# Biases of the attention's q, k and v taken off TensorE, in a three-layer decoder block on one core

## The reference

```
def _L0_attn_ref(x, Wq, bq, Wk, bk, Wv, bv, Wo, bo):
    q = (x @ Wq.T + bq).reshape(B, S, H, D)
    k = (x @ Wk.T + bk).reshape(B, S, H, D)
    v = (x @ Wv.T + bv).reshape(B, S, H, D)
    ...            # rotary turn of q and k by position
    qk = jnp.einsum('bshd,bstd->bsht', q, k) / jnp.sqrt(jnp.float32(D))   # heads against heads, per token
    att = jax.nn.softmax(qk, axis=-1)
    out = jnp.einsum('bsht,bstd->bshd', att, v)
    ...
    return out @ Wo.T + bo

x = _layernorm(x + _L0_attn_ref(x, ...))                  # attention
x = _layernorm(x + _L0_xattn_ref(x, ctx, ctx, ...))       # mLSTM over ctx: gates, decay matrix D, q-k product, norm
x = _layernorm(x + _L0_ffn_ref(x, ...))                   # 8 experts, one chosen per token, low rank
```

## Time and profile before

| | us |
|---|---|
| median of three runs | 1596.8 (1593.08 to 1603.48) |
| the profiled execution: its own time | 1598.22 |
| its span | 1596.5 |
| PE busy | 1506.4 (94%) |
| DVE busy | 1278.2 (80%) |
| ACT busy | 947.1 (59%) |
| POOL busy | 629.7 (39%) |
| mean granted TensorE clock | 0.973 of full |

### The profile page before, as it was taken

The page is one execution under the profiler, slowest core; times in us unless marked ns, Lnnn a source line. Parts: engine busy times, 40 slices in busy tenths (PEclk is TensorE's granted clock), DMA queues, the critical chain, the costliest instruction groups (busy, mean ns, idle before and its releaser), DMA issues.

```text
span 1596.5 us, 67819 instructions
## 1 busy us (share of the span) xinstructions
PE 1506.4 (94%) x27277; PEld 1194.9 (75%) x27404; DVE 1278.2 (80%) x3337; ACT 947.1 (59%) x2897; POOL 629.7 (39%) x975
## 2 busy tenths in 40 slices
PE   6889999999999999999999999999999999999964
PEld 5677777777777877777787777777777777777742
DVE  6567787788888888888888888888888888888764
ACT  3354656656665665666566566656656665665652
POOL 2233434434434443443444344344444434434431
PEclk8999999999999999999999999999999999999965
DMA  6232433333434333343333334333333433433310
GB/s 206 81 101 84 132 105 101 120 111 100 132 103 118 109 116 109 104 132 103 113 113 113 111 105 132 102 114 113 112 112 105 131 102 106 122 112 112 86 68 27
DMA packets 195143, 174.71 MB, mean 109 GB/s; under 512 B 141887, under 2 KB 143551, under 8 KB 186890
## 3 DMA queue, kind: packets, MB, share of 16 engines
q1 hardware_dynamic: 195082, 173.87, 36.3%
HBM read 139.76 MB, written 34.08 MB: 109 GB/s over the span
## 4 chain that ended last, share of the span: by engine, by line
PE 73%; DVE 18%; issue 5%; ACT 4%; DVEq 0%; POOL 0%; POOLq 0%
PE bank L386 13%; PE bank L387 12%; PE bank L389 12%; PE bank L378 6%; PE quad L440 5%; PE quad L453 5%; PE bank L548 5%; PE quad L500 4%; PE bank L482 4%; PE bank L535 4%; DVE w_sum L950 2%; DVE neg_max L941 2%; DVE ex L946 2%; DVE st L971 2%; ACT Hs L686 2%
## 5 line engine op out<-in xcount | busy, mean ns | idle before, releaser
L679 ACT ACTIVATE Dx<-Mb,a_col 128x128 f32<-128x128 f32 x1024 | 317.7, 388 | 4.1 <-DMA Mb<-m_rows 4.1
L820 POOL TENSOR_TENSOR ex<-ex,w_rec 128x512 f32<-128x512 f32 x64 | 67.1, 1048 | 510.7 <-DVE w_rec L955 510.7
L825 POOL TENSOR_SCALAR_AFFINE_SELECT Dx<-Dx 128x512 f32<-128x512 f32 x256 | 167.5, 679 | 88.4 <-ACT Dx L679 88.4
L1015 DVE SCALAR_TENSOR_TENSOR Dx<-quad,Dx 128x512 f32<-128x512 f32 x256 | 158.7, 681 | 4.4 <-POOL Dx L825 4.1
L721 ACT ACTIVATE ln<-ve 128x1 f32<-128x1 f32 x192 | 38.1, 199 | 197.0 <-DVE ve L976 197.0
L839 POOL TENSOR_TENSOR r<-r,lns_sb 128x512 f32<-128x512 f32 x64 | 82.6, 1290 | 173.2 <-DVE r L1038 106.2
L649 ACT ACTIVATE x1T<-bank 128x512 f32<-128x512 f32 x64 | 38.3, 599 | 149.0 <-PE bank L378 149.0
L386 PE MATMUL bank<-wq_high,x_high 128*128 128x512 f32 x256 | 115.1, 450 | 10.5 <-DVE wq_low L1161 8.5
L386 PE MATMUL bank<-wv_high,x_high 128*128 128x512 f32 x256 | 114.0, 445 | 1.5 <-issue 1.3
L386 PE MATMUL bank<-wk_high,x_high 128*128 128x512 f32 x256 | 114.0, 445 | 0.0
L453 PEld LDWEIGHTS quad<-PT,VG 32*32 32x32 f32 x8192 | 74.9, 103 | 51.9 <-issue 51.2
(11 more groups left out here) (164 smaller groups left out, 4168.5 us busy)
## 6 DMA issues: line engine op xcount, KB each, us to landing
Mb<-m_rows SPq DMA_DIRECT2D x64, 1024.0 KB, 4.7
xb<-in_x SPq DMA_DIRECT2D x256, 64.0 KB
cb<-in_ctx SPq DMA_DIRECT2D x64, 256.0 KB, 2.7
xr<-in_x SPq DMA_DIRECT2D x64, 256.0 KB, 2.7
v_rows<-v_sb SPq DMA_DIRECT2D x64, 256.0 KB, 2.4
VG<-v_rows SPq DMA_DIRECT2D x64, 256.0 KB, 3.9
out_dram<-yo SPq DMA_DIRECT2D x64, 256.0 KB, 2.8
Dx<-in_wq SPq DMA_DIRECT2D x4, 256.0 KB, 3.7
```

What stands on the lines that cost most here:

```text
L679: last = go(Dx[t.parity()][:, j, n, :], Mb[t.parity()][:, h, :], ACT.Exp, bias=a_col[t.parity()][:, h:h + 1], scale=-1.0)
L825: nc.gpsimd.affine_select(Dx[t.parity()][:, j], Dx[t.parity()][:, j], compare_op=ALU.is_ge, fill=0.0, base=0, pattern=[[0, CH], [1, P]], c ...
L1015: stt(out=Dx[t.parity()][:, j], in0=quad[:, j, :].rearrange("p (c n) -> p c n", n=P), scalar=float(D) ** -0.5, in1=Dx[t.parity()][:, j], o ...
```

## The change

- The bias matmuls are gone. For q and k, ACT writes the bias (spread over the 128 partitions in new tables `bias_bc`) into bank 4 ahead of the product (`p_seed_q`, `p_seed_k`), and the product's first matmul adds to what stands there (`first` is False). For v, the product starts its own accumulation, and POOL adds the bias to v_sb in place (`p_vb`); `store_v` waits for that.
- k moves from bank 6 to bank 4, so q and k of a tile use bank 4 in turn: seed of k waits for `QT_sb`, seed of the next q for `KT_sb`.
- F moves from bank 4 to bank 7 and in PE's order from after x1T to before QK; QK stands ahead of k.
- The wait for Hs moves from Y to O.
- `r_y` moves from DVE to POOL; POOL's r_r2 goes from the start of the next step to behind r_y2. On DVE the step ends with C x4 and then KT, and x_shift goes before a_x1.
- In the prologue: no splitting of the biases on DVE, three broadcast loads of 256 KB instead of three of 2 KB, 105 warm-up matmuls (into bank 4) instead of 68.

```diff
-WARM = 68
+WARM = 105
...
             def store_v(t):
-                sp.wait_ge(s.v_sb, upto(t))
+                sp.wait_ge(s.vb_sb, upto(t))
...
-            def bias(b, n):
-                mm(bank[b][:], ones_bf[:], bias3[:, n * E:(n + 1) * E], start=True, stop=False)
...
             def p_q(t):
...
                 pe.wait_ge(s.xlow_sb, upto(t))
-                edge(pe, t, (s.xhigh_sb, 0), (s.QT_sb, 1), (s.fn1_sb, 5))
-                bias(4, 0)
+                pe.wait_ge(s.seedq_sb, upto(t))
+                edge(pe, t, (s.xhigh_sb, 0))
                 product(4, x_high, x_low, 0, False).then_inc(s.q_ps, 1)
 
             def p_k(t):
...
-                pe.wait_ge(s.x2T_sb, upto(t, 4))
-                edge(pe, t, (s.xhigh_sb, 0), (s.xlow_sb, 0), (s.Hs_sb, 3), (s.y3_sb, 6), (s.LT_sb, 6))
-                bias(6, 1)
-                product(6, x_high, x_low, 1, False).then_inc(s.k_ps, 1)
+                pe.wait_ge(s.seedk_sb, upto(t))
+                edge(pe, t, (s.xhigh_sb, 0), (s.xlow_sb, 0))
+                product(4, x_high, x_low, 1, False).then_inc(s.k_ps, 1)
 
             def p_v(t):
...
-                bias(7, 2)
-                product(7, x_high, x_low, 2, False).then_inc(s.v_ps, 1)
+                product(7, x_high, x_low, 2, True).then_inc(s.v_ps, 1)
 
             def a_S(t):
-                for j in range(4):
-                    pe.wait_ge(s.C_sb[j], upto(t, 2))
+                pe.wait_ge(s.KT_sb, upto(t))
...
             def a_O(t):
                 pe.wait_ge(s.pads_set, PADS)
+                pe.wait_ge(s.Hs_sb, upto(t, 2))
...
             def m_gate(t):
-                pe.wait_ge(s.v_sb, upto(t, -1))
+                pe.wait_ge(s.fn1_sb, upto(t, 3))
...
             def x_F(t):
+                pe.wait_ge(s.v_sb, upto(t, -4))
                 pe.wait_ge(s.x2T_sb, upto(t))
-                pe.wait_ge(s.QT_sb, upto(t, -4))
...
-                    last = mm(bank[4][:, 0:NW], x2T[:, c, :], wx_sb[:, c, :], start=(c == 0), stop=(c == CH - 1))
+                    last = mm(bank[7][:, 0:NW], x2T[:, c, :], wx_sb[:, c, :], start=(c == 0), stop=(c == CH - 1))
...
             def x_Y(t):
                 pe.wait_ge(s.LT_sb, upto(t))
-                pe.wait_ge(s.Hs_sb, upto(t, -3))
...
             # PE step
                 if b.real():
                     a_proj(b)
+                if e.real():
+                    x_F(e)
+                if c.real():
+                    m_QK(c)
                 if a.real():
                     p_k(a)
-                if c.real():
-                    m_QK(c)
                 if b.real():
                     m_x1T(b)
-                if e.real():
-                    x_F(e)
                 if f.real():
                     x_LT(f)
...
             # ACT: p_seed_q first in the step, p_seed_k behind r_sq
+            def p_seed_q(t):
...
+                act.wait_ge(s.KT_sb, upto(t, 1))
+                go(bank[4][:], bias_bc[0][:], ACT.Copy, scale=float(D) ** -0.5).then_inc(s.seedq_sb, 1)
+
+            def p_seed_k(t):
...
+                act.wait_ge(s.QT_sb, upto(t))
+                go(bank[4][:], bias_bc[1][:], ACT.Copy).then_inc(s.seedk_sb, 1)
...
             # POOL: p_vb first in the step; r_y, r_y2, r_r2 before x_nm
+            def p_vb(t):
...
+                pool.wait_ge(s.v_sb, upto(t))
+                pool.wait_ge(s.acol_sb, upto(t, 2))
+                tt(v_sb[:], v_sb[:], bias_bc[2][:], ALU.add).then_inc(s.vb_sb, 1)
+
+            def r_y(t):
+                pool.wait_ge(s.hrs_sb, upto(t))
+                pool.wait_ge(s.x2_sb, upto(t, 1))
+                tt(r2[:].rearrange("p (c j d) -> p c j d", j=4, d=D),
+                   Hs[:, :, 0:P].rearrange("p c (j d) -> p c j d", d=D),
+                   h_rs[:].rearrange("p (c j) -> p c j", j=4).unsqueeze(3).broadcast_to([P, CH, 4, D]),
+                   ALU.mult).then_inc(s.y1_sb, 1)
...
             # DVE step
-                if d.real():
-                    r_y(d)
                 if b.real():
                     a_r1(b)
                     a_stats(b)
+                if e.real():
+                    x_shift(e)
+                if b.real():
                     a_x1(b)
+                if c.real():
+                    for j in (1, 3, 0, 2):
+                        m_C(c, j)
                 if a.real():
                     p_KT(a)
-                if c.real():
-                    for j in (1, 3, 0, 2):
-                        m_C(c, j)
-                if e.real():
-                    x_shift(e)
```

More of the change, by code:

```diff
@@ L240, in bass_decoder @@
             ve3_sb ln3_sb rs3_sb nm3_sb yo_sb""".split()
-        four = "Dx_sb Dm_sb C_sb w_in".split()
+        four = "Dx_sb Dm_sb C_sb w_in b_in".split()
         two = "x_in c_in r_in mb_in v_in".split()
@@ L251, in bass_decoder @@
                 [Mb[1][:, 4 * c:4 * c + 4, :].rearrange("p g n -> p (g n)") for c in range(CH)]]
-        bias_in = [t[0:1, :] for t in (y3[0], y3[1], yo)]
-        bias_rest = [t[0:1, :] for t in (x1[0], x1[1], x2[0])]
-        firsts = [(id_sb[:], ident), *[(bias_in[n], bqkv[:, n * E:(n + 1) * E]) for n in range(3)]]
         consts = [
@@ L379, in transposes @@
                 return last
-            def bias(b, n):
-                mm(bank[b][:], ones_bf[:], bias3[:, n * E:(n + 1) * E], start=True, stop=False)
             def product(b, high, low, n, first):
                 for c in range(CH):
-                    mm(bank[b][:], high[:, c, :], w_high[n][:, c, :], start=first and c == 0, stop=False)
-                    mm(bank[b][:], high[:, c, :], w_low[n][:, c, :], start=False, stop=False)
+                    mm(bank[b][:], high[:, c, :], w_high[n][:, c, :], start=first and c == 0, stop=False, skip_group_check=True)
+                    mm(bank[b][:], high[:, c, :], w_low[n][:, c, :], start=False, stop=False, skip_group_check=True)
                 for c in range(CH):
-                    last = mm(bank[b][:], low[:, c, :], w_high[n][:, c, :], start=False, stop=c == CH - 1)
+                    last = mm(bank[b][:], low[:, c, :], w_high[n][:, c, :], start=False, stop=c == CH - 1,
+                              skip_group_check=True)
                 return last
@@ L421, in p_v @@
                     pe.wait_ge(s.low_set, 2)
-                    pe.wait_ge(s.bias_step, 10)
                 pe.wait_ge(s.acol_sb, upto(t, 2))
                 edge(pe, t, (s.xhigh_sb, 0), (s.xlow_sb, 0))
-                bias(7, 2)
-                product(7, x_high, x_low, 2, False).then_inc(s.v_ps, 1)
+                product(7, x_high, x_low, 2, True).then_inc(s.v_ps, 1)
             def a_S(t):
-                for j in range(4):
-                    pe.wait_ge(s.C_sb[j], upto(t, 2))
-                edge(pe, t, (s.QT_sb, 0), (s.KT_sb, 0), (s.Ohigh_sb, 1), (s.Olow_sb, 1))
+                pe.wait_ge(s.KT_sb, upto(t))
+                edge(pe, t, (s.QT_sb, 0), *[(s.C_sb[j], 2) for j in range(4)], (s.Ohigh_sb, 1), (s.Olow_sb, 1))
                 for w in range(4):
@@ L477, in m_gate @@
             def m_gate(t):
-                pe.wait_ge(s.v_sb, upto(t, -1))
+                pe.wait_ge(s.fn1_sb, upto(t, 3))
                 pe.wait_ge(s.x1T_sb, upto(t))
+                edge(pe, t, (s.v_sb, -1))
                 edge(pe, t, (s.cT_sb, 0), (s.acol_sb, 1), (s.Hs_sb, 2))
@@ L557, in _ @@
             pe.wait_ge(s.center_set, 2)
-            for _ in range(WARM):
-                mm(bank[5][:, 0:P], ones_bf[:], ones_bf[:], start=True, stop=True)
+            for n in range(WARM):
+                last = mm(bank[4][:, n % 4 * P:(n % 4 + 1) * P], ones_bf[:], ones_bf[:], start=(n == 0), stop=True,
+                          skip_group_check=True)
+            last.then_inc(s.warm_ps, 1)
             pe.wait_ge(s.center_set, 12)
-            pe.wait_ge(s.first_in, FIRST_IN)
+            pe.wait_ge(s.first_in, 16)
             def step(a):
@@ L842, in r_r2 @@
                 pool.wait_ge(s.y2_sb, upto(t))
-                pool.wait_ge(s.x1_sb, upto(t, -1))
+                edge(pool, t, (s.x1_sb, 0))
                 tt(r2[:], r2[:], x1[t.parity()][:], ALU.add).then_inc(s.r2_sb, 1)
@@ L905, in step @@
                 if c.real():
+                    r_y(c)
                     r_y2(c)
+                    r_r2(c)
                 if f.real():
@@ L1060, in x_shift @@
                 edge(dve, t, (s.L_sb, 1), (s.fn2_sb, 1))
-                tt(fz[:], bank[4][:, 0:2 * nw], wx_shift[:, 0:2 * nw], ALU.subtract).then_inc(s.fz_sb, 1)
-                stt(out=f_n1[:], in0=bank[4][:, 2 * nw:NW], scalar=-2.0, in1=wx_shift[:, 2 * nw:NW],
+                tt(fz[:], bank[7][:, 0:2 * nw], wx_shift[:, 0:2 * nw], ALU.subtract).then_inc(s.fz_sb, 1)
+                stt(out=f_n1[:], in0=bank[7][:, 2 * nw:NW], scalar=-2.0, in1=wx_shift[:, 2 * nw:NW],
                     op0=ALU.mult, op1=ALU.add).then_inc(s.fn1_sb, 1)
```

65 lines of the change are left out of this document (26 added, 39 removed).

## The result

The changed kernel takes 1625.2 us (median, 1624.9 to 1625.8), beside 1597.1 for the kernel before: a ratio of 1.0171, 95% interval 1.0149 to 1.0193. The forecast was 1600, its range ended at 1620. It is slower, by more than the 1% that was set as the bound. Of the rivals C came near in time (1623), but not by what happened.

A forecast was written before the change was run, and what follows sets the result against it. PE, busy 94%, was taken to bound the kernel. From 1598.2, +6 for steps, +1.5 start and -3 tail gave 1602.7, 1601 as median, stated as 1600; the forecast's own range was 1584 to 1614, the overall range 1578 to 1620.

The forecast's parts named there:

- Rival C: POOL's longer queue ahead of the masks delays m_C and KT by 0.4 a step: 1623 us, chance 0.05.
- The three parts of a step: PE's step cut at S, v's first matmul and the projection's end: 9.50, 6.05 and 7.88 us.
- The bare price of bank 5: Between the transpositions of x1 and the next x, without F as cover: a new PE wait of 0.79 a step.
- The Hs wait: PE's wait before Y on ACT's Hs goes and doesn't come back at O: 0.28 a step.
- the seed of k fits: ACT's write between sq and f_e, in a gap of 0.50, sticks out by 0 to 0.1 us.
- v's bias on POOL costs nothing: A 1.29 us operation on POOL; v is read back only for O, so PE shows no delay.
- The start: 37 more warm-up matmuls against no bias splitting on DVE: +1.5 us, bounds 0 and +3.7.
- The tail: The last tile's r_y starts earlier on POOL than on DVE: -3 us, bounds -5 and 0.
- the large terms (0.51 and 0.28 against 0.79 and 0.10): Per PE step: bias matmuls save 0.51, Hs wait 0.28; bank 5 costs 0.79, and the step grows 0.10.
- rival B: Mb's load lands late, delaying Dx, v_sb and F: 0.27 more a step at a 5.1 landing, 1616 us, chance 0.14.
- "58 steps: +6": Filled part, about 130 to 1490 us: 58 steps of 23.43 instead of 23.33, +6 us, between -8 and +12.
- the order "KT, seed of q, x_high": The seed of q delays ACT's copy of x by about 0.4, covered as q comes 2.6 after S: no cost.

The follow-up runs named there:

- e2: The kernel before with F moved ahead of k in PE's queue, nothing else; 1640.6 us, one run.
- e11: The kernel before with only the Hs wait moved from Y to the O product of the next step; 1579.0 us, ratio 0.9881.
- e5: The changed kernel with v's bias on POOL behind the three masks and r_r2 at the head of the next step; 1630.8 us, ratio 1.0210.
- e18: e11 with 8 steps written out in place of 10; 1582.4 us, ratio 0.9905.
- e13: The kernel before with the biases of q, k and v left out and 98 warm-up matmuls in place of 68; 1585.5 us, ratio 0.9902.
- e8: The kernel before with 105 warm-up matmuls in place of 68, nothing else; 1895.2 us, one run.
- e10: The changed kernel with x1's transposition inside k, v's bias behind POOL's masks and x_high ahead of the seed of q; 1582.3 us, ratio 0.9904.
- e3: The changed kernel with 68 warm-up matmuls in place of 105; 1847.7 us, ratio 1.1572.
- e12: The changed kernel with 113 warm-up matmuls in place of 105; 1631.2 us, one run.
- e6: The changed kernel with r_y back on DVE, ahead of r1; 1732.5 us, ratio 1.0814.
- e16: e10 with 121 warm-up matmuls in place of 105; 1652.9 us, one run.
- e1: The changed kernel with x1's transposition between k's eighth and ninth matmul; 1629.5 us, ratio 1.0208.

## Why the prediction was wrong

**Right.** The three parts of a step within 0.04 each. The bare price of bank 5 (e2: 0.81, forecast 0.79). The Hs wait (e11: 0.30, forecast 0.28). That the seed of k fits and that v's bias on POOL costs nothing in the step as long as bank 5 sets it (e5).

**Right in number, not shown or by luck.** The start (+1.0, forecast +1.5): e2, e11 and e18 start as the kernel before does and reach tile 3 at 102.8, 105.8 and 104.1 where it takes 106.2, so +1.0 is within the scatter. The tail (-2.4, forecast -3): the last tile's r_y does start 2.4 earlier behind h_rs and r2 is 2.1 earlier, but from h_rs to the end it is 28.3 instead of 29.0 (29.0 also in e2, e11 and e18, all with r_y on DVE). So the move is worth 0.7; the other 1.7 lie ahead of h_rs, where e11 has 4.2 less than before.

**Mis-sized: the step.** The forecast had 23.43, with 0.10 over before and +6 for 58 steps. The shortest steps are 23.50 to 23.52. Three rests of 0.02, 0.04 and 0.03 add to 0.09, as much as the whole forecast difference: the sum of the large terms (0.51 and 0.28 against 0.79 and 0.10) nearly cancels, so its error rules. One of those terms is sized by e13: the bias matmuls are worth 0.45 a step, not 0.51. Over the loop's 50 steps the shortest step gives +10 where 5 was said. On top come 4 us by which the mean exceeds it, 3 of them in the steps in which F waits for v_sb. That is rival B, priced at 16 more for a landing of 5.1 in every step and given 0.14. B's limit of 4.83 was taken at F's first matmul; the weight load ahead of it already waits from about 4.6, below the median of 4.7. And a spread around the limit strikes every second step; it isn't all or nothing.

**Failed: "58 steps: +6".** This step took the steady step for all tiles from about 130 us on. Tiles 3 to 12 took 14.0 more, about 13 of it unforecast. The trace of before already had it: these nine steps take 8.7 more than nine of 23.32, with 9.8 us of "issue" stops, and I read no row of that stretch. (The 0.73 on "issue" in the earlier trace rows is not one of them: xT starts 0.10 behind the end of ACT's copy of x1T, so it is the handover, as it was read.) The stops from 107 to 340 grew from 9.8 to 17.0 us, and the granted clock fell to 0.97. e13, which has nothing else of the change, shows such a loss too (+7.2), and e8 that the place of the code alone can bring it (tiles 3 to 10: +13.7). Both are changed in the changed kernel, and in e13. Three shifts of e10 and one of the changed kernel (e3) moved the sum by 3 at most, which speaks for the missing matmuls, and e12 by 6; how much is due to the shorter steps and how much to the place is open. Over nine of their own mean loop steps, tiles 3 to 12 take 17 to 27 us more in the variants without bias matmuls, and 7 to 14 in those with them (before 8.7, e2 7.1, e11 12.5, e18 14.2). Left aside are e6, whose loop is itself held up, and e3, e8 and e16, whose loops have stops.

**Rival C** had the right picture (DVE and POOL longer side by side) and the wrong consequence: KT ended at S - 0.78 instead of S - 1.0 and nothing waited for it. The loop over POOL binds only when bank 5 no longer does (e1), or when it is itself lengthened (e6). I had costed the order "KT, seed of q, x_high" at nothing because q comes 2.6 later; its real reader is x_low and behind it gs, HT and neg_max.

So of the +26.8: about +13 unforecast stops and clock in the written-out steps, +10 longer base step (5 forecast), +4 in the steps above it (3 by the late Mb), +1 start, -2.4 tail, +1 forecast in the written-out steps.
